# Graph layer kernel on one core: the x rows loaded tile by tile, the word matmuls, loads and slot branch in another order, and mix·W1 of three output tiles ahead of a branch and a correction

## The chip, the core and the metric

The kernel runs on one core of a Trainium2 chip. The metric is the device time of one execution in microseconds; less is better. Matmuls run on TensorE (PE), elementwise work on VectorE (DVE) and ScalarE (ACT), gathers by index are issued by GpSimd (POOL), and most DMAs by SyncE (SP).

## The reference, cut to what matters

N = 1354 nodes with H = 512 features; `adj` is a sparse 0/1 matrix with ones on the diagonal; 10,000 index pairs of which few hit an edge of `adj`.

```python
# layer 0: attention over adj; only pairs (sub, obj) that are edges get a score other than 0
q = (x[sub] @ Wq.T + bq);  k = (x[obj] @ Wk.T + bk)            # 8 heads of 64
scores = zeros.at[:, sub, obj].set((q * k).sum(-1) / 8);  scores = where(adj == 0, -inf, scores)
scores[:, i, i] = 1e-7
x = layernorm(x + (softmax(scores).sum(0) / 8) @ x)
# layer 1: a graph convolution
x = layernorm(x + adj @ (x @ W1) + b1)
```

## The kernel before

Rows are taken in T = 11 tiles of 128 (the last has 74 rows). Nearly every softmax row is uniform, so layer 0 is a neighbour sum `adj @ x` scaled per row, and the few pairs that are edges (at most 64 "slots") are corrected by a small branch of work. All engines run lists written out by hand; semaphores join them. The stages are these.

**Loads.** SP issues the tiles of `adj_t` (704 KB each) into a ring of three in `stage`; load t waits until the cast of tile t−3 is done (`adj_cast`). ACT casts each to fp16 (`cast_adj`, L622). x comes in three loads of three tiles and two of one. SP also waits for `edges_split` (from DVE's `split_left`), stores the left-over pair indices to DRAM, waits until they are stored, and loads them again broadcast over the partitions (`hot`, `cols`). POOL meanwhile looks up the first LOOKED = 44 of 80 pair columns in `adj`, one gather each.

**Words and sums.** For each tile, `words(t)` on PE (L1116, 11 matmuls of 129 columns) packs the adjacency bits and counts the neighbours; DVE's `fold(t)` (L773 to L778) takes them out of PSUM and `coefs(t)` makes scale factors. `words(t)` waits for the cast of tile t and, since it has two banks, for fold t−2. `sum_neighbours(i)` (L1125, 22 matmuls of 512 columns) sums tile i. On DVE `add_sums(i)` (L849 and the moments L793, L794) takes it; ACT takes the root (L627), then casts two more adjacency tiles, then normalises (L658) and scales (L661); DVE makes the low half (`low_x1`, L862), and scale and shift (`scale_shift_of`, L798, L799). A turn i of ACT's loop thus has the casts 4+2i and 5+2i between the root and the normalisation of tile i. In the first two sums PE works in blocks of three x tiles as x arrives.

**Looks and picks.** After the last sums, `look(n)` (PE, L1139) multiplies a table with 500 pairs; `pick(n)` (DVE, L812) takes it; a look waits for the pick two before it. `select` (L1188) sums the picks into one word for each pair.

**Mix and the slot branch.** `mix_rows(a, b)` is x1ᵀ·adjᵀ (L1179): 12 units of 11 rows, a row being two matmuls, of 512 columns in the units 0 to 7 and of 330 in 8 to 11. Between its rows stand by hand the PE steps of the slot branch: numbering, compaction (L1212), spread (L1217), transposes of gathered rows, projections (L1234), dots, `scores_spread` (L1252), `mixed` (L1256), the transposes of the change (L1260) and the change times W1 (L1267). DVE and ACT do the small steps between. ACT evicts a mix unit (`mix_high`, L666), DVE makes its low half (`mix_low`, L818).

**Branch and output.** All engines load `count_i` into a register and branch over a general path that is not taken (L248). Then `transform` (L1279: 12 matmuls mix·W1; L1287: 2 of the correction) makes the output tiles over six banks; DVE and ACT normalise them and SP stores them.

## Time and profile before

| | |
|---|---|
| median of 3 runs | 214.2 us (212.41 to 219.76) |
| the profiled execution | 212.14 us, of which the span from first to last instruction is 210.4 |
| PE busy | 175.6 us (83%) |
| DVE / ACT / POOL busy | 119.9 / 70.0 / 75.6 us |
| mean granted TensorE clock | 0.929 |

```profile
PE   4489720999999999969999999997589699999920
DVE  2569505776777677794621571059984226556660
ACT  6376123578533333370211111108022101332350
PEclk9958955699999999999999999999799999999995
DMA  5993299998798899120110060000000001122220
```

Each digit is a fortieth of the span (5.3 us), in tenths of busy time; PEclk is the granted clock, 5 being the lower of its two levels (1.2 GHz) and 9 about the upper (2.4 GHz). PE is busy nearly all the time except in the slices 5 to 7, a stretch near 145 to 157 us, and the end.

### The profile page before, as it was taken

Reading aid. Unit: us, or ns where it says so; the run is one execution under the profiler, and the core shown is the slowest. Engines: PE = TensorE matmul, PEld = TensorE weight load, DVE = VectorE, ACT = ScalarE, POOL = GpSimd, SP = SyncE. Lnnn points to the kernel's source line nnn. Section 1 sums busy time; section 2 is a strip of 40 time slices with the busy share of each in tenths; the row PEclk is TensorE's granted clock in tenths of the full one; section 3 lists DMA queues with packets and bytes.
Section 4 is the critical chain, followed back from the end, with each engine's and each line's share of the span. In section 5 each row is a group of like instructions: output and inputs, shape, how many; then the busy total and the mean of one; then the engine's idle time right before and its main releaser. Section 6 shows DMA issues by size and latency. Waiting matters only on the chain.

```text
span 210.4 us, 2793 instructions
## 1 busy us (share of the span) xinstructions
PE 175.6 (83%) x995; PEld 94.6 (45%) x995; DVE 119.9 (57%) x371; ACT 70.0 (33%) x119; POOL 75.6 (36%) x87
## 2 busy tenths in 40 slices
PE   4489720999999999969999999997589699999920
PEld 4444320655555444435444446954255344444520
DVE  2569505776777677794621571059984226556660
ACT  6376123578533333370211111108022101332350
POOL 5687887878785562301882150000000000000000
PEclk9958955699999999999999999999799999999995
DMA  5993299998798899120110060000000001122220
GB/s 162 377 346 82 29 379 332 310 341 201 174 324 272 292 289 309 52 52 3 1 1 1 0 181 9 0 3 2 0 0 0 5 9 50 65 86 100 97 106 29
DMA packets 14594, 26.66 MB, mean 127 GB/s; under 512 B 5459, under 2 KB 5620, under 8 KB 14445
## 3 DMA queue, kind: packets, MB, share of 16 engines
q1 hardware_dynamic: 9436, 22.46, 31.9%
q10 hardware_dynamic: 3152, 2.90, 4.5%
q0 software_dynamic: 1984, 1.05, 4.0%
q8 instruction: 10, 0.16, 0.3%
q14 instruction: 12, 0.09, 0.2%
HBM read 16.70 MB, written 9.65 MB: 125 GB/s over the span
## 4 chain that ended last, share of the span: by engine, by line
PE 65%; DVE 17%; DMA 7%; ACT 4%; issue 3%; SPq 1%; ACTq 0%; DVEq 0%
PE acc L1179 18%; PE acc L1125 14%; PE acc L1279 10%; PE tr L1125 7%; DMA x_sb<-in_x 5%; PE tr L1116 3%; PE tr L1234 3%; PE tr L1279 2%; DVE xs L766 2%; DMA stage<-in_adj_T 2%; DVE st L793 2%; PE acc L1287 2%; ACT adjT L622 1%; PE tr L1267 1%; PE acc L1188 1%
## 5 line engine op out<-in xcount | busy, mean ns | idle before, releaser
L570 POOL DMA_INDIRECT ed_adj<-in_adj,ed_idx x44 | 55.2, 1255 | 19.0 <-issue 16.0
L1179 PE MATMUL acc<-adjT,x1s 128*128 128x512 f16 (+3 forms) x264 | 54.3, 360 | 0.0
L1125 PE MATMUL acc<-xs,adjT 128*128 128x512 f16 (+1 forms) x176 | 41.3, 392 | 0.7 <-DVE xs L766 0.7
L1179 PEld LDWEIGHTS acc<-adjT,x1s 128*128 128x128 f16 (+1 forms) x264 | 25.5, 100 | 24.6 <-issue 1.8
L1125 PEld LDWEIGHTS acc<-xs,adjT 128*128 128x128 f16 (+1 forms) x176 | 17.4, 100 | 21.5 <-DVE xs L766 1.8
L1279 PE MATMUL acc<-whl,xs 128*128 128x512 f16 (+1 forms) x108 | 23.5, 367 | 2.1 <-issue 2.1
L1116 PE MATMUL tr<-bit_eye,adjT 128*128 128x129 f16 x121 | 11.5, 260 | 12.8 <-ACT adjT L622 12.8
L666 ACT ACTIVATE xs<-acc 128x512 f16<-128x512 f32 (+1 forms) x12 | 6.5, 546 | 43.5 <-PE acc L1179 43.5
L622 ACT CAST adjT<-stage 128x1408 f16<-128x1408 f32 x11 | 14.9, 1363 | 12.6 <-DMA stage<-in_adj_T 12.3
L1116 PEld LDWEIGHTS tr<-bit_eye,adjT 128*128 128x128 f16 x121 | 9.9, 118 | 15.6 <-ACT adjT L622 10.9
L1279 PEld LDWEIGHTS acc<-whl,xs 128*128 128x128 f16 x108 | 10.5, 98 | 13.9 <-issue 2.4
L587 POOL DMA_INDIRECT found<-in_adj,top_i x8 | 10.6, 1323 | 15.5 <-DVE top_i L904 13.3
L1125 PE MATMUL tr<-xs,adjT 128*128 128x512 f16 (+1 forms) x66 | 15.6, 394 | 0.0
L818 DVE SCALAR_TENSOR_TENSOR xs<-acc,xs 128x512 f16<-128x512 f32 (+1 forms) x12 | 7.4, 624 | 10.8 <-ACT xs L666 10.6
L627 ACT ACTIVATE st<-st,co 128x1 f32<-128x1 f32 x11 | 3.2, 293 | 22.2 <-DVE st L794 22.1
L1125 PEld LDWEIGHTS tr<-xs,adjT 128*128 128x128 f16 (+1 forms) x66 | 6.6, 102 | 8.0 <-issue 1.1
L766 DVE SCALAR_TENSOR_TENSOR xs<-x_sb,xs 128x512 f16<-128x512 f32 x11 | 6.9, 685 | 4.0 <-ACT xs L632 4.0
L711 ACT ACTIVATE y<-y,st 128x512 f32<-128x512 f32 x6 | 4.9, 812 | 12.3 <-DVE st L799 12.3
L793 DVE BATCH_NORM_STATS2 st<-y 128x6 f32<-128x512 f32 x12 | 8.3, 694 | 0.4
L1073 DVE SCALAR_TENSOR_TENSOR y<-acc,x_sb 128x512 f32<-128x512 f32 x5 | 3.5, 691 | 8.7 <-PE acc L1287 8.7
L627 ACT ACTIVATE st<-st,eps 128x1 f32<-128x1 f32 x13 | 3.7, 283 | 12.8 <-DVE st L794 12.6
L862 DVE SCALAR_TENSOR_TENSOR x1s<-x_sb,x1s 128x512 f16<-128x512 f32 x11 | 7.5, 681 | 0.4 <-ACT x1s L661 0.4
(236 smaller groups left out, 209.2 us busy)
## 6 DMA issues: line engine op xcount, KB each, us to landing
stage<-in_adj_T SPq DMA_DIRECT2D x11, 704.0 KB, 7.7
adjT_dram<-adjT SPq DMA_DIRECT2D x11, 352.0 KB, 3.0
x_sb<-in_x SPq DMA_DIRECT2D x3, 768.0 KB, 11.5
sums_dram<-y ACTq DMA_DIRECT2D x6, 256.0 KB, 5.9
out<-y SPq DMA_DIRECT2D x6, 256.0 KB, 2.0
sums_dram<-xd ACTq DMA_DIRECT2D x5, 256.0 KB, 3.3
hot<-row_dram SPq DMA_DIRECT2D x1, 1125.0 KB, 8.8
stage<-in_L_gnn_weight SPq DMA_DIRECT2D x1, 1024.0 KB, 6.5
```

Source lines behind the costliest of these rows:

```text
L570: nc.gpsimd.indirect_dma_start(out=ed_adj[0:EP, c:c + 1], out_offset=None, in_=adj_flat, in_offset=bass.IndirectOffsetOnAxis(ap=ed_idx[0:E ...
L587: nc.gpsimd.indirect_dma_start(out=found[0:EP, c:c + 1], out_offset=None, in_=adj_flat, in_offset=bass.IndirectOffsetOnAxis(ap=top_i[0:EP, ...
L622: nc.scalar.copy(adjT[:, :, t * P:(t + 1) * P], stage[:, t % RING, :].rearrange("p (k i) -> p k i", k=T)).then_inc(adj_cast, 1)
L627: return nc.scalar.activation(s[:, 10:11], s[:, 7:8], ACT.Sqrt, bias=floor)
L766: V.scalar_tensor_tensor(xs[:, 1, t, :], x_sb[:, t, :], XS, xs[:, 0, t, :], ALU.mult, ALU.subtract).then_inc(x_lo, 1)
L793: step(V.bn_stats(s[:, 0:6], v))
L818: V.scalar_tensor_tensor(mix[:, 1, u % KF, i:j], mix_bank(u)[:, 0:j - i], 1.0 / XS, mix[:, 0, u % KF, i:j], ALU.mult, ALU.subtract).then_i ...
L862: V.scalar_tensor_tensor(x1s[:, 1, i, :], x_sb[:, i, :], XS, x1s[:, 0, i, :], ALU.mult, ALU.subtract).then_inc(x1_lo, 1)
L1116: last = mm(tr[t % 2][:, 0:P + 1], adjT[:, k, t * P:(t + 1) * P], bit_eye[:, k, :], start=(k == 0), stop=(k == T - 1))
L1125: last = mm(sum_bank(i)[:, :], adjT[0:width[k], k, i * P:(i + 1) * P], xs[0:width[k], half, k, :], start=(k == 0 and half == 0), stop=(k = ...
L1179: ins = mm(mix_bank(u)[:, 0:j - i], x1s[0:width[k], half, k, f * P:(f + 1) * P], adjT[0:width[k], k, i:j], start=(k == 0 and half == 0), s ...
L1279: mm(bank, mix[:, a, k, t * P:(t + 1) * P], whl[:, b, k, columns], start=(k == 0 and n == 0), stop=False)
```

## The change

- x is loaded in 11 single tiles, and the load of the left-over pairs goes behind x and adjacency tile 2. The adjacency loads 3, 4 and 5 no longer stand behind SP's wait for `edges_split`; tile 6 stands behind it, tile 7 behind the `hot` broadcast.
- DVE makes all 11 low halves of x, then folds and coefs of tiles 0 and 1, then `split_left` and `edge_bits`, then the loop. Fold 2 moves into turn 0, folds 3 and 4 into turn 2, and so on (`FOLDS_AFTER`); `low_x1(i-1)` comes before `scale_shift_of(i)`.
- PE runs words 2 before the sums of tile 2, words 3 and 4 before those of 3, 5 and 6 before 4, and so on (`WORDS_BEFORE`).
- LOOKED goes from 44 to 40, so that 40 pair columns are left over (before 36), 10 looks instead of 9 and 40 selects instead of 36. Two looks each follow the sums of tiles 7, 8 and 9; four stand in the mix rows, each two rows apart.
- The slot branch: some mix rows stand elsewhere between its PE steps; the part of the DVE chain that needs only `gsub` (through the moments of `kk`) moves ahead of the scores, its root with it, so that ACT loads the Exp table before the scores are there and no mix unit's eviction stands between; the scaling by `rep` moves to the two-element coefficients.
- `transform` becomes `base` (mix·W1) and `correct`; the base of output tiles 0, 1 and 2 runs before the branch over the general path, and the general path (not taken) clears and remakes them.

```diff
-LOOKED = 44
+LOOKED = 40
-LOOKS_AFTER = {T - 4: range(0, 1), T - 3: range(1, 3), T - 2: range(3, 5), T - 1: range(5, 6)}
+WORDS_BEFORE = {2: (2,), 3: (3, 4), 4: (5, 6), 5: (7,), 6: (8, 9), 7: (10,)}
+FOLDS_AFTER = {0: (2,), 2: (3, 4), 3: (5, 6), 4: (7,), 5: (8, 9), 6: (10,)}
+LOOKS_AFTER = {T - 4: range(0, 2), T - 3: range(2, 4), T - 2: range(4, 6)}
+LOOKS_IN_MIX = {2: 6, 4: 7, 6: 8, 8: 9}
+EARLY = 3
...
             load_adj(0)
-            for g in range(3):
-                if g == 1:
-                    load_adj(1)
-                sp.dma_start(x_sb[:, 3 * g:3 * g + 3, :],
...
+            for t in range(3):
+                load_x(t)
+            load_adj(1)
+            for t in range(3, T):
+                load_x(t)
             load_adj(2)
+            sp.dma_start(left_i, pairs_left).then_inc(left_loaded, 16)
+            load_adj(3)
+            load_adj(4)
+            load_adj(5)
             sp.wait_ge(edges_split, 2)
...
-            load_adj(3)
-            load_adj(4)
+            load_adj(6)
             sp.wait_ge(row_stored, 16)
             sp.dma_start(hot[:, :], row_dram.partition_broadcast(P)).then_inc(row_spread, 16)
-            load_adj(5)
+            load_adj(7)
...
             for i in range(T):
                 add_sums(i)
-                if i + LEAD + 1 < T:
-                    fold(i + LEAD + 1)
-                if i + 2 < T:
-                    coefs(i + 2)
-                scale_shift_of(i)
+                for t in FOLDS_AFTER.get(i, ()):
+                    fold(t)
+                if 1 <= i < T - 1:
+                    coefs(i + 1)
                 if i >= 1:
                     low_x1(i - 1)
+                scale_shift_of(i)
...
             last.then_inc(keys_ready, 1)
-            mix_high(7)
+            act.wait_ge(slot_moments, 1)
+            root(st[:, 0], eps[:]).then_inc(slot_root, 1)
 
             nc.scalar.activation(table_loader[:, 1:2], eps[:], ACT.Exp)
             act.wait_ge(exps_in, 1)
             nc.scalar.activation(score, score, ACT.Exp).then_inc(exps_done, 1)
             nc.scalar.activation(table_loader[:, 2:3], eps[:], ACT.Sqrt)
+            mix_high(7)
             mix_high(8)
-            act.wait_ge(slot_moments, 1)
-            root(st[:, 0], eps[:]).then_inc(slot_root, 1)
...
-            mix_rows(118, UNITS * T)
-
-            with overflow(pe):
-                general_pe(pe)
+            mix_rows(117, UNITS * T)
...
+            for t in range(EARLY):
+                pe.wait_ge(mix_lo, (4, 4, 9)[t])
+                base(out_bank(t)[:, :], t, everything).then_inc(based, 1)
+
+            with overflow(pe):
+                general_pe(pe, base)
```

On PE, at the start of the sums (`tr<-bit_eye,adjT` is a tile's words, `xs,adjT` a tile's sums of 22 matmuls), before:

```order
L1125 MATMUL acc<-xs,adjT 128x512 x38
L1116 MATMUL tr<-bit_eye,adjT 128x129 x44
L1125 MATMUL tr<-xs,adjT 128x512 x22
L1116 MATMUL tr<-bit_eye,adjT 128x129 x11
L1125 MATMUL acc<-xs,adjT 128x512 x22
L1116 MATMUL tr<-bit_eye,adjT 128x129 x11
L1125 MATMUL acc<-xs,adjT 128x512 x22
```

The same place of the changed kernel:

```order
L1131 MATMUL acc<-xs,adjT 128x512 x38
L1122 MATMUL tr<-bit_eye,adjT 128x129 x11
L1131 MATMUL tr<-xs,adjT 128x512 x22
L1122 MATMUL tr<-bit_eye,adjT 128x129 x22
L1131 MATMUL acc<-xs,adjT 128x512 x22
L1122 MATMUL tr<-bit_eye,adjT 128x129 x22
L1131 MATMUL acc<-xs,adjT 128x512 x22
```

Four tiles' words stood between the first sums and those of tile 2; now one does, and the others stand one or two sums later.

On PE, around the branch over the general path (`whl,onehot` is the change times W1, `whl,xs` 12 matmuls of mix·W1, `stackR,stackL` the correction), before, with the general path left out between the two pieces:

```order
L1267 MATMUL tr<-whl,onehot 64x512 x12
L1179 MATMUL acc<-adjT,x1s 128x330 x28
L248 TENSOR_LOAD count_i
L248 ISA x2
L248 COMPARE_AND_BRANCH
L277 UNCONDITIONAL_BRANCH
```

```order
L1272 UNCONDITIONAL_BRANCH
L1279 MATMUL acc<-whl,xs 128x512 x12
L1287 MATMUL acc<-stackR,stackL 128x512 x2
L1279 MATMUL tr<-whl,xs 128x512 x12
L1287 MATMUL tr<-stackR,stackL 128x512 x2
```

The changed kernel ahead of the branch, and behind it:

```order
L1270 MATMUL tr<-whl,onehot 64x512 x12
L1183 MATMUL acc<-adjT,x1s 128x330 x30
L1279 MATMUL acc<-whl,xs 128x512 x12
L1279 MATMUL tr<-whl,xs 128x512 x12
L1279 MATMUL acc<-whl,xs 128x512 x12
L252 TENSOR_LOAD count_i
L252 ISA x2
L252 COMPARE_AND_BRANCH
```

```order
L1299 UNCONDITIONAL_BRANCH
L1291 MATMUL acc<-stackR,stackL 128x512 x2
L1291 MATMUL tr<-stackR,stackL 128x512 x2
L1291 MATMUL acc<-stackR,stackL 128x512 x2
L1279 MATMUL acc<-whl,xs 128x512 x12
```

36 matmuls of 512 columns moved ahead of the register load and the branch; none was added on the path that is taken.

## Rows read from the trace of the kernel before

**Rows 1.** The page: the span.

```profile
span 210.4 us, 2793 instructions
```

**Rows 2.** Waits of PE: waiting line, awaited, us in total, times, longest.

```profile
PE tr L1116 <- ACT adjT L622: 12.8, 3, 5.3
...
PE tr L1139 <- DVE hot L812: 2.2, 2, 1.7
PE acc L1279 <- issue: 2.1, 1, 2.1
```

**Rows 3.** Timeline of SP: start us, us, what was issued.

```profile
23.54 0.32 SPq L510 DMA_DIRECT2D row_dram<-row  x1
...
24.32 0.83 SPq L497 DMA_DIRECT2D stage<-in_adj_T  x2
25.19 0.42 SPq L515 DMA_DIRECT2D hot<-row_dram  x1
```

**Rows 4.** Chain that ended last: start us, us, what.

```profile
28.48 1.37 ACT adjT L622
...
39.25 5.56 PE tr L1125 x22
44.81 0.65 PE tr L1116 x11
45.46 4.75 PE acc L1125 x22
```

**Rows 5.** Timeline of PE: the last words before the gap.

```profile
24.40 0.81 PE L1116 MATMUL tr<-bit_eye,adjT 128*128 128x129 f16 x11
```

**Rows 6.** Busy time in a stretch: PE, PEld, DVE, ACT, POOL, then clock, DMA share, GB/s.

```profile
145.00:157.00 12.00, 7.59 (x37) 3.79 (x36) 11.03 (x34) 3.29 (x8) 0.00 (x0) 0.86 0.00 0
```

**Rows 7.** DMA issues: KB each, us from issue to landing.

```profile
hot<-row_dram SPq DMA_DIRECT2D x1, 1125.0 KB, 8.8
```

**Rows 8.** Timeline of ACT: casts, a root, a normalisation.

```profile
20.69 1.37 ACT L622 CAST adjT<-stage 128x1408 f16<-128x1408 f32 x1 [0.60 <-DMA stage<-in_adj_T]
50.32 0.81 ACT L658 ACTIVATE x_sb<-xd,st 128x512 f32<-128x512 f32 x1
51.17 0.63 ACT L661 ACTIVATE x1s<-x_sb 128x512 f16<-128x512 f32 x1
```

**Rows 9.** Timeline of DVE: first and last of the 14 instructions of one turn.

```profile
50.24 0.75 DVE L849 SCALAR_TENSOR_TENSOR xd<-acc,co,x_sb 128x512 f32<-128x512 f32 x1 [1.39 <-PE acc L1125]
...
54.17 0.61 DVE L805 TENSOR_SCALAR hot<-hot,row_no 128x1500 f16<-128x1500 f16 x1
```

**Rows 10.** Timeline of PE: the long stretch of mix rows.

```profile
96.27 19.60 PE L1179 MATMUL acc<-adjT,x1s 128*128 128x512 f16 x90
```

**Rows 11.** Timeline of ACT: the Exp table and the Exp of the scores.

```profile
143.52 1.28 ACT L685 ACT_TABLE_LOAD   x1
...
144.92 0.63 ACT L687 ACTIVATE wraw<-wraw 128x536 f32<-128x536 f32 x1
```

**Rows 12.** Timeline of DVE: scores done, and the sum behind the Exp.

```profile
143.35 0.72 DVE L997 TENSOR_TENSOR wraw<-wraw 128x536 f32<-128x536 f32 x1
...
146.66 0.65 DVE L1019 TENSOR_REDUCE wraw<-wraw 128x8 f32<-128x512 f32 x1
```

**Rows 13.** Timeline of PE: the end of the slot branch, and the mix rows before the branch instruction.

```profile
149.43 1.55 PE L1256 MATMUL tr<-wraw 64*128 64x512 f32 x2 [3.48 <-DVE wraw L1031]
...
156.87 0.46 PE L1260 MATMUL tr<-ident,wraw 64*128 64x64 f32 x4 [0.93 <-DVE wraw L1050]
...
161.75 4.10 PE L1179 MATMUL acc<-adjT,x1s 128*128 128x330 f16 x28
```

**Rows 14.** Instructions of the branch: engine, ns min/median/max, start us.

```profile
L248 SPq COMPARE_BRANCH  x1: 50/50/50, 120.5 to 120.5; - x1
...
L248 PEldq TENSOR_LOAD <-count_i x1: 483/483/483, 163.2 to 163.2; - x1
...
L248 PEldq COMPARE_BRANCH  x1: 3845/3845/3845, 164.0 to 164.0; - x1
```

More of the change, by code:

```diff
@@ L325, in general_pe @@
             pe.wait_ge(turn, FINISHED)
+            for t in range(EARLY):
+                base(out_bank(t)[:, :], t, slice(0, H))
         def general_act(act):
@@ L640, in _ @@
             cast_adj(0)
-            high_x(0)
+            for t in range(3):
+                high_x(t)
             cast_adj(1)
-            high_x(1)
-            high_x(2)
-            high_x(3)
-            for t in range(2, LEAD + 1):
-                cast_adj(t)
+            for t in range(3, T):
+                high_x(t)
+            cast_adj(2)
+            cast_adj(3)
             for i in range(T):
@@ L652, in _ @@
                 act.dma_start(sums_dram[i * P:(i + 1) * P, 0:H], y4(i)).then_inc(y_stored[i % YS], 16)
-                for t in range(LEAD + 1 + 2 * i, min(LEAD + 3 + 2 * i, T)):
+                for t in range(4 + 2 * i, min(6 + 2 * i, T)):
                     cast_adj(t)
@@ L671, in _ @@
             nc.scalar.mul(bias_hl[:, 0], bias_row[:, :], WS).then_inc(bias_split, 1)
-            for u in range(7):
+            for u in range(6):
                 mix_high(u)
@@ L827, in _ @@
             step(V.scalar_tensor_tensor(diag_bit, aii_all, -1.0, power, ALU.mult, ALU.mult))
[L828 removed]
+            for t in range(T):
                 split_x(t)
[L830 to L837 removed]
+            for t in range(2):
+                fold(t)
+                coefs(t)
             split_left()
[L839 to L840 removed]
             edge_bits()
@@ L880, in _ @@
                     pick(n)
+            pick(LOOKS_IN_SUMS)
             low_x1(T - 1)
-            for n in range(LOOKS_AFTER[T - 1].stop, LOOKS):
+            for n in range(LOOKS_IN_SUMS + 1, LOOKS):
                 pick(n)
@@ L964, in _ @@
             V.tensor_copy(xoT, tr[2][:, 0:KF * SLOTS]).then_inc(xoT_ready, 1)
+            dve.wait_ge(gsub_in, 16)
+            aii = gsub[:, H + 1:H + 2]
+            plain, off = slot[:, 7:8], slot[:, 9:10]
+            step(V.tensor_tensor(off, gsub[:, H:H + 1], aii, ALU.subtract))
+            b = small[:, 24:32]
+            own, den, both = b[:, 0:1], b[:, 1:2], b[:, 2:3]
+            step(V.tensor_scalar(own, aii, -A0, 1.0, ALU.mult, ALU.add))
+            step(V.tensor_scalar(den, off, A0, 1.0, ALU.mult, ALU.add))
+            step(V.tensor_tensor(both, den, own, ALU.add))
+            step(V.reciprocal(b[:, 3:4], den))
+            step(V.tensor_tensor(b[:, 4:5], both, b[:, 3:4], ALU.mult))
+            step(V.tensor_scalar(kk, gsub[:, 0:H], b[:, 4:5], None, ALU.mult))
+            norm_a, norm_b = st[:, 0], st[:, 1]
+            moments(norm_a, kk).then_inc(slot_moments, 1)
             mix_low(6)
@@ L976, in _ @@
             last.then_inc(qk_read, 1)
+            dve.wait_ge(slot_root, 1)
+            step(scale_shift(norm_a))
+            step(V.tensor_scalar(norm_a[:, 8:10], norm_a[:, 8:10], rep, None, ALU.mult))
+            V.tensor_scalar(kk, kk, norm_a[:, 8:9], norm_a[:, 9:10], ALU.mult, ALU.add).then_inc(dve_step, 1)
+            steps += 1
             sc = small[:, 4:12]
@@ L1153, in _ @@
             sum_neighbours(1, range(9, T))
-            for t in range(2, LEAD + 2):
-                words(t)
             for i in range(2, T):
-                if i + LEAD < T:
-                    words(i + LEAD)
+                for t in WORDS_BEFORE.get(i, ()):
+                    words(t)
                 if i >= 3:
@@ L1190, in select @@
                     last.then_inc(selected, 1)
-            looks = LOOKS_AFTER[T - 1].stop
-            mix_rows(0, 2)
-            for n in range(looks, LOOKS):
-                look(n)
-                mix_rows(2 * (n - looks) + 2, 2 * (n - looks) + 4)
-            for n in range(looks):
+            for n in range(9):
+                mix_rows(n, n + 1)
+                if n in LOOKS_IN_MIX:
+                    look(LOOKS_IN_MIX[n])
+            for n in range(LOOKS_IN_SUMS):
                 select(n)
-            mix_rows(2 * (LOOKS - looks) + 2, 9)
-            for n in range(looks, LOOKS):
+            mix_rows(11, 13)
+            for n in range(LOOKS_IN_SUMS, LOOKS):
                 select(n)
-            mix_rows(11, 20)
+            mix_rows(13, 20)
             mix_rows(9, 11)
@@ L1222, in _ @@
             last.then_inc(xobj_T, 1)
-            mix_rows(77, 78)
+            mix_rows(73, 76)
             pe.wait_ge(xsub_in, 16)
```

106 lines of the change are left out of this document (44 added, 62 removed).

## The prediction

> **What bounds the kernel now.** I read the page's slices first, then the waits of PE, then the chain that ended last. The execution took 212.14 us, of which the span is 210.4 [rows 1]; the 1.74 us around it I keep. PE is busy in almost every slice outside a few holes, and the chain runs mostly over PE, so a hole closed is time won, as long as no other engine takes its place. The largest waits in the table are 12.8 us for ACT's casts (three of them), 2.2 us for DVE's picks and 2.1 us of "issue" before the first output tile [rows 2]. The timeline of PE adds 3.48 and 0.93 us late in the slot branch [rows 13].
>
> The casts are late because of SP's list, not because of the bus. SP has adjacency tile 3 behind its wait for the split pairs: it stores them at 23.54, so tile 3 is issued only at 24.32 [rows 3] and cast at 28.48 [rows 4], while tile 2 was cast at 20.69 [rows 8]. Tile 4's cast stands on ACT behind the root of tile 0, and that root waits for DVE, which must first fold tile 3. PE did words 2 from 24.40 [rows 5] and began the sums of tile 2 at 39.25, and those took 5.56 us where the later ones take 4.75 [rows 4].
>
> **The first gap: -13.5 us.** In the new list tiles 3 to 5 don't wait for the split, and only words 2 stands ahead of the sums of tile 2. From 24.40 to 39.25 are 14.85 us; in them lay four tiles' words, which are still to be done and cost 0.65 us each at the full clock [rows 4], 2.6 in all. That leaves 12.25. The sums of tile 2 come at 4.75 instead of 5.56: 0.8. Single x tiles let the first products start earlier; the first sums of 38 matmuls were bound by PE, so this is small: I take 0.5, with 0 and 1 as ends.
>
> **What is late next: +4.4 us.** The cover of 13 us is gone, and now the loads are asked for earlier than they can come. A load of 704 KB issued on an idle queue landed in 4.1 us (24.32 to the cast at 28.48). Two such loads and the 1125 KB of `hot` were done 8.8 us after 25.19 [rows 3, 7], at 34.0: the 1829 KB behind tile 3 took 5.5 us, about 330 KB/us. So an adjacency tile takes 2.1 us, and `hot`, now 1250 KB, 3.8. Tile 2 at 20.7, tile 3 at 22.8, tile 4 at 24.9, tile 5 at 27.0, tile 6 (issued near 25, behind the split) at 29.1, `hot` at 33, tile 7 behind it at 35.1. Two stores of 256 KB that ACT issues meanwhile take 0.8 each: 36.7.
>
> Tile 7's cast stands on ACT between root 1 and the normalisation of tile 1. It ends near 38.1; normalisation and scaling, 0.81 and 0.63 [rows 8], bring 39.6. On DVE `low_x1(1)` now stands ahead of scale and shift of tile 2, so the DVE list stands still: queued behind it are add_sums 3 and folds 5 and 6. A turn of DVE is 4.5 us (50.24 to the end of the row at 54.17 [rows 9]) and PE's turn 5.4, so DVE makes up only about 1 us a turn, less where two folds stand in one. By these steps PE, which would be at words 7 at 41.3, waits for fold 5 until 42.9 (1.6); at words 9 for fold 7 (1.4); at look 0 for the table, which now comes in turn 6 (1.3). Together about 4.4. The slope is 1 us for each us that tile 7 lands later; if it lands by 32.5 there is no wait at all. Ends: 0 and +9 (tile 7 and its followers 4 to 5 us later, as when the stores and the broadcast of `cols` share the bus).
>
> **Looks: -0.9.** Four looks in the mix rows stand one row further apart. The last waits for the pick two before it, which stands behind `low_x1(10)`: 1.0 of wait in place of 2.2. One look and four selects more cost 0.3. The flags must be back from POOL when PE has done the mix rows behind the selects; two rows fewer lie there (0.43 each: 19.60 us for 90 matmuls [rows 10]), which the earlier end of the selects pays. Four lookups fewer lie beside this work and cost or give nothing.
>
> **Slot branch: -3.3.** The scores are written at 143.35 + 0.72 = 144.1, but Exp started at 144.92, since the table load began only at 143.52 [rows 11, 12], behind the eviction of mix unit 7. DVE then did the `gsub` part and reached the sum at 146.66. Now both lie in the cover of the projections: Exp from 144.1, 0.63 long, the sum at 144.8, 1.9 earlier. PE had 3.48 us of wait there [rows 13] to take it from. From L1256 to L1260 are 7.4 us [rows 13], set by DVE; three passes over 512 elements leave that chain and small ones come in: -1.0, between -0.5 and -1.5. One mix row less stands ahead of the spread of scores: -0.4. The clock was 0.86 from 145 to 157 [rows 6], after the long wait; waits of 1.4 and 1.3 us remain, shorter than the 2.1 [rows 2] behind which the outputs ran at full pace, so I expect the upper level, 2.4 GHz. This changes no sum here, since DVE sets it.
>
> **Bases ahead of the branch: -2.0.** The wait of 2.1 before L1279 is the branch. TensorE's sequencer loaded the register at 163.2, while matmuls ran until 165.85 (161.75 + 4.10), and its branch instruction lasted 3845 ns from 164.0 [rows 13, 14]; SP's took 50 ns [rows 14]. So load and branch need 4.7 us, of which 2.65 were covered by about 18 queued matmuls of 0.146 us. Ahead of them now are matmuls of 0.216 us: the same 18 cover 3.9, a gap of 0.8. In longer matmuls the sequencer gains more lead, and 36 of them, 7.8 us, stand there; I take the gap as 0.1. Ends: 2.1 won or nothing. The outputs 0 to 2 then come in a bunch, later for DVE, but DVE's part of an output (add, moments, scale and shift) is a piece of its turn of 4.5 us [rows 9], an estimated 2, against PE's 14 matmuls of 0.216, 3.0, and there are six banks; what follows the last output matmul stays as it is.
>
> The Trainium skill ("Runtime: NRT & Kernel Launch", Instruction fetch mechanics) says that a taken branch to a target outside the fetched pages must wait for a DMA of the target page. A fetch would run beside queued matmuls; by that rule, which the row of 3845 ns bears out, the gap goes and the sum stands.
>
> **The sum.** 212.14 - 13.5 + 4.4 - 0.9 - 3.3 - 2.0 = 196.8 us. The median of the runs before is 2.1 above the profiled execution and the lowest run 0.3 above it; I leave the number as it is.
>
> **Rivals.** *No late wait*: tile 7 lands by 33. For it: loads before tile 2 were asked for in one go. Against: the 330 KB/us and 1250 KB of `hot` ahead of it. 196.8 - 4.4 = 192.4. *The branch waits for an empty array*: its 3845 ns end 2.04 after the last matmul, which fits that as well. Then nothing is won: 198.8. *A longer wait of DVE*: tiles 7 to 9 come 4 to 5 us later: 201 to 203. *Slower than before*: DVE's `split_left` now waits for the pairs, whose load stands behind x and tile 2, and behind it stand add_sums 0 and the whole list. By the same rate they land at 21, when DVE gets there; each us beyond it costs one. From 15 us late the gain of 15.3 is gone; at 24 us late it would be 196.8 + 24 = 220.8. Nothing in the rows speaks for such a delay of so small a load.
>
> **Chances and range.** Forecast 0.52; no late wait 0.15; branch not covered 0.17; longer DVE wait 0.12; slower 0.01; and 0.03 that gains are lost in places I don't see, to within 2% of before (about what a measurement of this kernel can tell from no change). Faster by over 2% is thus 0.95, within 0.03, slower 0.02. The forecast alone spans 194.5 to 199. From 191.5 to 203 leaves out less than 2 in 10: the low end is no late wait with the better start, the high end the longer wait of DVE.
>
> **What would show it.** Right: PE without a hole from 24 to 41 us, then waits for `fold_in` and for the table of 1 to 2 us each; a cast of ACT near 37 that waited for its load; the sums' end near 78 (before 87); Exp within 0.1 us of the scores; the wait before L1256 about 1.4; the branch instruction of TensorE as long as before, with no hole in the matmuls beside it. Wrong: waits of PE for casts again, a hole of 2 us right behind the bases, or waits of 3 us and more for DVE in the sums.

## The result, and the profile after

The changed kernel takes 202.6 us (median of 4 runs, 201.5 to 204.6), the kernel before beside it 217.0 (median of 4 runs, 212.4 to 220.4); the ratio is 0.948, 95% interval 0.933 to 0.963. The medians in this text contain executions that were slower whatever the kernel did, and the ratios leave them out: without them the kernel before shows about 213. Faster, as forecast, but 5.8 us above the 196.8 that was predicted, at the upper end of the range. The profiled execution took 201.47 us:

```profile
span 199.7 us, 2808 instructions
```

The waits of PE (columns as in [rows 2]). The 12.8 us for ACT's casts are 0.6 now. Besides 2.9 us for POOL at the start, which both kernels have, the largest that are left are the fold in the sums, DVE's split of the last x tile, the two of the slot branch and the branch itself:

```profile
PE tr L1122 <- DVE fold_in L786: 3.6, 1, 3.6
...
PE acc L1131 <- DVE xs L778: 2.6, 2, 1.8
PE tr L1259 <- DVE wraw L1040: 1.6, 1, 1.6
PE tr L1263 <- DVE wraw L1056: 1.5, 1, 1.5
PE tr L1145 <- DVE hot L824: 1.0, 1, 1.0
PE acc L1291 <- issue: 0.8, 1, 0.8
PE tr L1122 <- ACT adjT L634: 0.6, 2, 0.4
```

The timeline of PE in the sums, and from their end (79.17) to the numbering, PE's first step for the slots (L1209, at 110.18). L1122 are words, L1131 sums, L1183 mix rows, L1145 looks, L1192 selects:

```profile
20.61 1.75 PE L1131 MATMUL acc<-xs,adjT 74*128 74x512 f16 x6 [1.75 <-DVE xs L778]
22.74 1.37 PE L1122 MATMUL tr<-bit_eye,adjT 128*128 128x129 f16 x11 [0.38 <-ACT adjT L634]
23.90 5.50 PE L1131 MATMUL tr<-xs,adjT 128*128 128x512 f16 x22
...
45.13 1.02 PE L1122 MATMUL tr<-bit_eye,adjT 128*128 128x129 f16 x11 [3.64 <-DVE fold_in L786]
45.94 6.42 PE L1131 MATMUL tr<-xs,adjT 128*128 128x512 f16 x22
...
84.99 0.37 PE L1145 MATMUL tr<-hot,table 128*128 128x500 f16 x1 [1.00 <-DVE hot L824]
85.20 1.53 PE L1192 MATMUL acc<-ones,hot 128*125 128x1 f16 x24
86.59 1.87 PE L1183 MATMUL acc<-adjT,x1s 128*128 128x512 f16 x4
88.25 1.81 PE L1192 MATMUL acc<-ones,hot 128*125 128x1 f16 x16
89.93 20.41 PE L1183 MATMUL acc<-adjT,x1s 128*128 128x512 f16 x86
110.18 0.17 PE L1209 MATMUL acc<-flag,below 125*128 125x8 f16 x1
```

The same two places in the kernel before, in its timeline of PE (what follows the last sums there is a look):

```profile
86.95 0.38 PE L1139 MATMUL tr<-hot,table 128*128 128x500 f16 x1
...
115.70 0.17 PE L1206 MATMUL acc<-flag,below 125*128 125x8 f16 x1
```

Sums 2 begin at 23.90, where they began at 39.25 [rows 4], and PE is through with the sums 7.8 us earlier (79.17; before 86.95). Then it loses 2.3 of them again: 31.0 us to the numbering where it took 28.8. The stretches (columns as in [rows 6]) say why; the clock fell to its lower level, 1.2 GHz, around the selects. PE is busy throughout these four; just ahead of them, at 84, lies its wait of 1.0 us:

```profile
86.00:88.00 2.00, 2.00 (x17) 1.17 (x16) 0.92 (x3) 0.00 (x0) 0.00 (x0) 0.63 0.04 8
88.00:90.00 2.00, 2.00 (x19) 1.80 (x18) 0.00 (x0) 0.00 (x0) 0.00 (x0) 0.50 0.00 0
90.00:92.00 2.00, 2.00 (x6) 0.64 (x6) 1.56 (x8) 0.00 (x0) 0.00 (x0) 0.50 0.00 0
92.00:94.00 2.00, 2.00 (x8) 0.80 (x7) 0.97 (x9) 0.00 (x0) 1.16 (x1) 0.66 0.00 0
```

The timeline of ACT: the cast of the last x tile (the one before it is cast at 14.99), and of adjacency tile 7.

```profile
19.20 0.63 ACT L643 ACTIVATE xs<-x_sb 128x512 f16<-128x512 f32 x1 [3.58 <-DMA x_sb<-in_x]
...
39.29 1.36 ACT L634 CAST adjT<-stage 128x1408 f16<-128x1408 f32 x1 [5.77 <-DMA stage<-in_adj_T]
```

The timeline of SP: three adjacency loads hold it from 9.16 until 23.04, since tile 5 waits for the cast of tile 2. The stores of the split pairs come at 25.04 ([rows 3] has 23.54), and the broadcast into `hot` at 27.90:

```profile
25.04 0.31 SPq L523 DMA_DIRECT2D row_dram<-row  x1
...
27.90 0.34 SPq L527 DMA_DIRECT2D hot<-row_dram  x1
```

What the stores waited for from 23.04 on is DVE's split, and `hot` waited for the stored rows (SP's waits, columns as in [rows 2]):

```profile
SPq L523 <- DVE col L765: 2.0, 1, 2.0
SPq L527 <- DMA row_dram<-row: 1.8, 1, 1.8
```

DVE's timeline has the reason: its split stands behind the low half of the last x tile, for whose cast it sat idle for 3.51 us; the split's last instruction (L765) ends at 25.01.

```profile
19.86 0.69 DVE L778 SCALAR_TENSOR_TENSOR xs<-x_sb,xs 128x512 f16<-128x512 f32 x1 [3.51 <-ACT xs L643]
```

### The profile page after: what moved, and what is told of

It is laid out like the page before. It is cut to its first block, busy times and chain, and to the rows that moved or that the text cites. A ratio compares the mean times of both kernels' runs of the same rounds, so it can differ in the third digit from the quotient of the medians.

```text
span 199.7 us, 2808 instructions
## 1 busy us (share of the span) xinstructions
PE 176.2 (88%) x1000; PEld 94.4 (47%) x1000; DVE 120.0 (60%) x373; ACT 70.0 (35%) x119; POOL 71.3 (36%) x83
## 4 chain that ended last, share of the span: by engine, by line
PE 62%; DVE 18%; DMA 6%; issue 6%; SPq 3%; ACT 3%; DVEq 0%
PE acc L1183 20%; PE acc L1279 10%; PE acc L1131 10%; DMA x_sb<-in_x 6%; PE tr L1131 5%; PE tr L1237 4%; PE tr L1279 3%; DVE st L805 2%; SPq L509 2%; PE acc L1291 2%; PE acc L1192 1%; PE tr L1122 1%; PE tr L1270 1%; DVE xd L854 1%; DVE x1s L867 1%
## 5 line engine op out<-in xcount | busy, mean ns | idle before, releaser
L582 POOL DMA_INDIRECT ed_adj<-in_adj,ed_idx x40 | 50.1, 1252 | 18.8 <-issue 15.7
L1183 PE MATMUL acc<-adjT,x1s 128*128 128x512 f16 (+3 forms) x264 | 55.6, 365 | 0.0
L1131 PE MATMUL acc<-xs,adjT 128*128 128x512 f16 (+1 forms) x176 | 40.1, 381 | 2.6 <-DVE xs L778 2.6
L1183 PEld LDWEIGHTS acc<-adjT,x1s 128*128 128x128 f16 (+1 forms) x264 | 25.6, 101 | 25.2 <-issue 4.2
L1131 PEld LDWEIGHTS acc<-xs,adjT 128*128 128x128 f16 (+1 forms) x176 | 16.7, 98 | 22.8 <-DVE xs L778 4.2
L1131 PE MATMUL tr<-xs,adjT 128*128 128x512 f16 (+1 forms) x66 | 16.8, 417 | 0.0
L599 POOL DMA_INDIRECT found<-in_adj,top_i x8 | 11.4, 1423 | 12.5 <-DVE top_i L910 10.4
L1122 PE MATMUL tr<-bit_eye,adjT 128*128 128x129 f16 x121 | 9.6, 238 | 4.2 <-DVE fold_in L786 3.6
L1122 PEld LDWEIGHTS tr<-bit_eye,adjT 128*128 128x128 f16 x121 | 8.5, 107 | 6.9 <-ACT adjT L634 5.9
L1131 PEld LDWEIGHTS tr<-xs,adjT 128*128 128x128 f16 (+1 forms) x66 | 7.1, 108 | 8.8 <-issue 2.7
L643 ACT ACTIVATE xs<-x_sb 128x512 f16<-128x512 f32 x11 | 6.6, 624 | 4.3 <-DMA x_sb<-in_x 4.1
```

Of the source, the lines that this page charges most:

```text
L582: nc.gpsimd.indirect_dma_start(out=ed_adj[0:EP, c:c + 1], out_offset=None, in_=adj_flat, in_offset=bass.IndirectOffsetOnAxis(ap=ed_idx[0:E ...
L599: nc.gpsimd.indirect_dma_start(out=found[0:EP, c:c + 1], out_offset=None, in_=adj_flat, in_offset=bass.IndirectOffsetOnAxis(ap=top_i[0:EP, ...
L1122: last = mm(tr[t % 2][:, 0:P + 1], adjT[:, k, t * P:(t + 1) * P], bit_eye[:, k, :], start=(k == 0), stop=(k == T - 1))
L1131: last = mm(sum_bank(i)[:, :], adjT[0:width[k], k, i * P:(i + 1) * P], xs[0:width[k], half, k, :], start=(k == 0 and half == 0), stop=(k = ...
L1183: ins = mm(mix_bank(u)[:, 0:j - i], x1s[0:width[k], half, k, f * P:(f + 1) * P], adjT[0:width[k], k, i:j], start=(k == 0 and half == 0), s ...
```

## The experiments

All are edits of the changed kernel unless said otherwise. A bracket behind a time holds its ratio to the kernel before and the 95% interval of that ratio; 0.010 is about 2 us. Where two times are compared across chips, their ratios to the kernel before are the better guide; the medians of it beside them were 212.7 to 218.6.

**The changed kernel again**, as the base for the runs beside it.

> The changed kernel as it is, as the measure for the runs beside it. Theory: span near 199.7 as in its first profile (201.5 us), with one wait of PE of 3.6 us for a fold in the sums, and the granted clock at its lower level for about 7 us around the selects (86 to 94 us in the first profile). Rival: the clock fell there by chance; then this run shows the upper level there and 3 us less from the last sums to the numbering (31.0 us in the first profile, 28.6 in the kernel before).

Measured 201.9 us (0.947, 0.938 to 0.955), so some 202. Its profiled execution repeats the fold wait (3.3), the split wait (2.8), both waits of the slot branch and the low clock at the selects.

**The last x tile in two loads, of 64 and 10 rows.**

```
- sp.dma_start(x_sb[0:width[t], t, :], rows(x, t))           # t = 10: 74 rows
+ sp.dma_start(x_sb[0:64, t, :], x[t*P:t*P+64, :]); sp.dma_start(x_sb[64:LAST, t, :], x[t*P+64:N, :])
```

> One edit: the last x tile, of 74 rows, is loaded in two pieces, of 64 and of 10 rows. Theory: its load ran on 2 of the 16 DMA engines (the Trainium skill, 'DMA: Bandwidth & Descriptors', says that the number of engines is the largest up to 16 that divides the rows: 2 for 74, 16 for 64, 10 for 10), which is why it landed at 19.2 us, 4 us behind the tile before it; now it lands by 16.5, PE's wait of 1.8 us before the last rows of the first sums goes, and adjacency tile 2 is cast 2 us or more earlier. Since the later wait for tile 7 is set by the queue, 0 to 2 us of it show at the end. Rival: it is late because it is last in the queue: it lands at 18.5 or later again, no change.

Measured 198.0 us (0.931, 0.921 to 0.940), profiled 196.04. ACT's timeline: both last x tiles are cast at 15.00 in one go, tile 2 at 17.47, tile 7 at 35.96:

```profile
15.00 1.26 ACT L647 ACTIVATE xs<-x_sb 128x512 f16<-128x512 f32 x2 [0.60 <-DMA x_sb<-in_x]
17.47 1.36 ACT L638 CAST adjT<-stage 128x1408 f16<-128x1408 f32 x1 [1.21 <-DMA stage<-in_adj_T]
...
35.96 1.36 ACT L638 CAST adjT<-stage 128x1408 f16<-128x1408 f32 x1 [5.36 <-DMA stage<-in_adj_T]
```

In SP's timeline of this run the stores of the split pairs stand at 21.88 and the broadcast into `hot` at 24.61.

So one load of 148 KB had delayed everything behind it: on ACT the cast of tile 2, on DVE the low half of the last x tile and the split behind it, with that the stores (25.04 to 21.88) and `hot`, by 3.3 us. From the issue of `hot` to the cast of tile 7 it takes 11.4 us in either kernel (39.29 - 27.90, 35.96 - 24.61). The Trainium skill ("DMA: Bandwidth & Descriptors", Why a DMA increments its semaphore by 16 and not by 1) says that a transfer runs on the largest number of engines up to 16 that divides its outermost size: 2 for 74 rows, 16 for 64. The trace agrees: the same bytes in pieces of 64 and 10 rows are cast 3.6 us earlier (15.63 against 19.20). In the five kernels of this study with the split tile its cast starts at 15.6 to 17.0, in the other eleven that were changed at 18.8 to 20.3. That the gain comes from the number of engines and not from there being two loads, no run separates. The end of the sums is 2.2 us earlier in this profiled execution (76.96); the rest of the 5.4 us between 201.47 and 196.04 is mostly that the clock did not fall at the selects here.

The fold wait doesn't shrink, though, since PE is earlier by as much (PE's timeline):

```profile
41.79 0.82 PE L1126 MATMUL tr<-bit_eye,adjT 128*128 128x129 f16 x11 [3.34 <-issue]
```

**The small load of the left pairs at the head of SP's list** instead of behind tile 2.

```
+ sp.dma_start(left_i, pairs_left)
  load_adj(0)
  ...
  load_adj(2)
- sp.dma_start(left_i, pairs_left)
```

> One edit: the load of the left-over pairs (40 rows of 1 KB) stands ahead of adjacency tile 0 again, as in the kernel before. It asks why adjacency tile 0 was cast at 8.3 us in the kernel before and at 5.3 to 5.9 in the changed one. Theory A: this small load delays the tile behind it by 3 us: the cast comes at 8 us again. Theory B: it was the x load of three tiles behind it: the cast stays below 6.5 us.

A single execution, 202.25 us. Tile 0 was cast at 7.72 instead of 5.29, and words 0 followed at 9.23 (7.09). The fifteen profiled executions without these 39 KB ahead of it have that cast at 5.29 to 6.93, so they cost the first tile 0.8 to 2.4 us. The kernel before has 8.33, so this is a large part of why the changed kernel starts earlier than I had priced.

**Adjacency tile 7 ahead of the broadcast of the rows.**

```
  load_adj(6)
+ load_adj(7)
  sp.wait_ge(row_stored, 16)
  sp.dma_start(hot, ...)
- load_adj(7)
```

> One edit: adjacency tile 7 is issued ahead of the broadcast of the left-over pairs instead of behind it. Theory: PE's wait of 3.6 us for a fold, and the lower clock behind it (1.5 us on the sums of tile 5), come from the cast of tile 7 that stands on ScalarE ahead of a normalisation and waited for its load until 39.3; now the load lands near 33, the wait goes, and the time is 4 to 5 us less. Rival: the bus is full, and the broadcast, now 2 us later, or tiles 8 and 9 hold DVE and PE as long: within 1 us of the changed kernel.

Measured 202.5 us (0.953, 0.948 to 0.958): no gain, as the rival had it. Tile 7 was cast at 36.72, 2.6 us earlier, but tile 8 only at 46.32, and the wait went there. PE's timeline:

```profile
54.85 1.35 PE L1122 MATMUL tr<-bit_eye,adjT 128*128 128x129 f16 x11 [5.80 <-DVE fold_in L786]
55.99 7.28 PE L1131 MATMUL acc<-xs,adjT 128*128 128x512 f16 x22
```

**Both broadcasts behind adjacency tile 9** (on top of the split x tile).

```
- load_adj(6); store rows, then hot; load_adj(7); cols; load_adj(8), load_adj(9), load_adj(10)
+ load_adj(6), load_adj(7), load_adj(8), load_adj(9); hot; cols; load_adj(10)
```

> Two edits on the changed kernel: the last x tile in two loads (as x10_split) and the two broadcasts of the left-over pairs issued behind adjacency tile 9 instead of around tile 7. Theory: the queue is full from 24 to 46 us, and what counts is which load stands first; with both broadcasts behind, tiles 7 to 9 land 3 to 6 us earlier, the wait of PE for a fold (3.3 us) goes and the lower clock behind it, so it is 3 to 5 us below x10_split. Rival: DVE then waits for the broadcast in turn 3 (before turns 3 to 5 use it), and the lists stand as long: within 1 us of x10_split or above it.

Measured 197.8 us (0.924, 0.913 to 0.935), the same as with the split x tile alone. Tiles 7, 8 and 9 were cast at 33.62, 36.45 and 39.34, tile 10 after a wait of 5.14 at 47.41, and PE waited 2.50 for the fold behind it. Moving bytes about in SP's list moves the wait; it doesn't remove it.

**ACT's casts behind the normalisation**, on top of three other edits (the kernel `best_so_far`, below): in every turn (first), and in all turns but 0 (second).

```
  root(i)
- cast_adj(4 + 2 * i), cast_adj(5 + 2 * i)
  normalise x1(i), scale x1s(i)
+ cast_adj(4 + 2 * i), cast_adj(5 + 2 * i)      # second: only for i > 0
```

> best_so_far with ACT's casts of a turn moved behind the normalisation and scaling of that turn, so that a cast that waits for its load no longer holds up the low part, DVE and its fold. Theory A (the wait of 3.3 us for fold 5 comes from ACT's order: DVE idles about 5 us on low_x1(1) while the cast waits): the wait goes, 3 us less than best_so_far, 193.5. Theory B (the loads are late on their own account and PE has used up its reserve of work): the fold wait shrinks by 1 at most and comes back as a wait for words 8 or 9, same time as best_so_far. A cast that stands 1.5 us later on ACT delays words by up to 1.5 us; that is the price in either.

> best_so_far with ACT's casts behind the normalisation in turns 1 to 3 only; in turn 0 tiles 4 and 5 are cast first, as in the changed kernel. Theory A (the fold wait of 3.1 to 3.6 us comes from the cast of tile 7 standing ahead of the normalisation, and the wait of 2.5 for cast 4 in norm_first from the cast standing behind it): neither wait, and the sums behind at full clock, 3 to 4 us less than 193.9: 190. Theory B (the loads of tiles 7 to 10 are what is late): the wait comes back before words 7 or 8, and the time stays within 1 of 193.9.

The first form measured 193.8 us (0.911, 0.905 to 0.918), against 194.0 of its base: no gain in time. The fold wait of 3.1 is gone, so it did come from ACT's order: in the changed kernel DVE stands idle 5.36 us ahead of `low_x1(1)` (42.07), which needs the scaling that ACT did behind the cast of tile 7. But cast 4 now stands behind the normalisation of turn 0, and that opened a wait of its own, with the low clock behind it:

```profile
28.54 1.06 PE L1130 MATMUL tr<-bit_eye,adjT 128*128 128x129 f16 x11 [2.48 <-ACT adjT L642]
29.39 6.39 PE L1139 MATMUL acc<-xs,adjT 128*128 128x512 f16 x22
```

The second form measured 193.0 us (0.907, 0.898 to 0.915), which can't be told from the first by these runs; I had expected 190. In PE's timeline no sums ran at the lower clock any more, but waits came back piecemeal, 4.1 us in three: 1.35 for a cast ahead of the words at 27.56, 0.96 and 1.77 for folds ahead of those at 40.55 and 48.53.

**The first gap, half undone twice**: SP's list as before from tile 3 on (`pairs_first`), and three tiles' words ahead of sums 2 on PE (`words_early`; the kernel before has four).

```
- load_adj(3), load_adj(4), load_adj(5); stores; load_adj(6); hot; load_adj(7); cols; load_adj(8) ...
+ stores; load_adj(3), load_adj(4); hot; load_adj(5); cols; load_adj(6) ...          # pairs_first
```

```
- WORDS_BEFORE = {2: (2,), 3: (3, 4), 4: (5, 6), 5: (7,), 6: (8, 9), 7: (10,)}
+ WORDS_BEFORE = {2: (2, 3, 4), 3: (5,), 4: (6,), 5: (7,), 6: (8, 9), 7: (10,)}     # words_early
```

> The changed kernel with SP's list as before from adjacency tile 3 on: tiles 3 and 4 behind the stores of the split pairs, tile 5 behind the broadcast of the rows, 6 to 10 behind that of the columns. PE's, ACT's and DVE's orders stay as changed. Prediction's theory (the casts were late because of SP's list): most of the 13.5 us comes back; at least 8 us slower than the changed kernel, 210. Rival (it was the order of the words on PE: sums 2 no longer stand behind words 3 to 6): tile 3 is cast at about 28.5, when sums 2 end anyway, tile 4 at about 32, so a wait of 3 us before sums 3 and 1 to 2 before sums 4, while the late wait for fold 5 goes: 0 to 3 us slower, 202 to 205.

> The changed kernel with words 2, 3 and 4 ahead of the sums of tile 2, then one tile's words ahead of each of sums 3 to 5, as the kernel before had it at the start; SP's list as changed. Theory A (the order of the words carries most of the 13.5 us): words 4 can't start before cast 4, at 29.4 in the changed kernel, or before fold 2, which DVE does behind add_sums 0; so sums 2 start at about 30.5 in place of 23.9, but they then stand behind three tiles' words that were due anyway (1.3 us): 5 us slower, 207; the wait for fold 5 shrinks, which gives back up to 3. Theory B (the list alone had carried it): less than 1.5 us slower.

Measured 206.0 us (0.973, 0.963 to 0.983) and 203.3 us (0.954, 0.946 to 0.961), against 202 of the changed kernel. The prediction's sentence "the casts are late because of SP's list" falls for the most part: with the old list sums 2 still start at 22.86, and PE waits 5.8 us ahead of words 3 and 4, and 2.18 for a fold at 45.42 (`pairs_first`):

```profile
22.86 4.91 PE L1129 MATMUL tr<-xs,adjT 128*128 128x512 f16 x22
31.99 1.37 PE L1120 MATMUL tr<-bit_eye,adjT 128*128 128x129 f16 x11 [4.23 <-ACT adjT L632]
34.91 1.37 PE L1120 MATMUL tr<-bit_eye,adjT 128*128 128x129 f16 x11 [1.55 <-ACT adjT L632]
```

With the words early and the new list, sums 2 start at 31.84 behind cast 4 (wait 4.29), and then one wait of 2.18 at 40.03 stands in place of the 3.64. Undoing the list costs 4 us (5 by the ratios), the words about 1, which these intervals can't tell from nothing; what either costs early is in part paid back late. Either one of the two thus closes most of the gap. No run undoes both at once, so that the two together carry the 13.5 us is argued, not shown.

**The selects**, set apart in the mix rows four by four (`selects_apart`), and all forty in a row (`selects_row`).

```
  for n in range(6): select(n)                  # 24 one-column matmuls
- mix_rows(11, 13)                              # selects_row: these rows behind the second group
  for n in range(6, 10): select(n)              # 16
```

```
+ mix_rows(n, n + 1); look(...); select(n)      # selects_apart, n = 0 to 5
+ mix_rows(5 + n, 6 + n); select(n)             # n = 6 to 9
```

> One edit: the 40 selects (matmuls of one column) stand in ten groups of four, each behind a mix row, instead of as 24 and 16 with two rows between. Theory: the lower clock around 86 to 94 us came from the selects standing together right behind a wait; apart, it stays at the upper level and the time is 3 us less. Rival 1: the clock fell for the wait of 1.0 us before the last look alone: no change. Rival 2: chance: it varies from run to run in both kernels.

> The changed kernel with the two mix rows between the two groups of selects moved behind them: 40 one-column matmuls in a row. Theory A (a string of one-column matmuls keeps the array so little busy that the clock falls): the granted clock falls to the lower level right behind or in them in each profiled execution; from the sums' end to the numbering 31 us or more, where it was 28.0 without a fall and 26.5 with the selects apart; the time 1 us above the changed kernel, which has the fall in most executions already: 203. Theory B (the wait of 1.0 before look 9 does it, which all have): no difference from the changed kernel, 28 to 31 us by the execution.

Measured 198.9 us (0.934, 0.928 to 0.940) and 200.6 us (0.940, 0.925 to 0.954). Set apart they save some 3 us. From the sums' end to the numbering all profiled executions give:

| selects | executions | sums' end to numbering |
|---|---|---|
| in groups, clock falls | after, changed_again, adj7_first, words_early | 31.0 each |
| in groups (selects_row: in one row), clock falls for less | hot_behind9, base_behind, load_hoisted, left_first, selects_row | 29.4 each |
| in groups, no fall | x10_split, pairs_first, chain_behind | 28.0 to 28.2 |
| apart, no fall | selects_apart, best_so_far, norm_first, norm_second | 26.5 each |

So the fall costs 3.0 or 1.4 us for the same instructions, and it was there in 9 of 12 executions with the selects in strings and in none of 4 with them apart. Apart, the stretch is another 1.5 us shorter (28.0 to 26.5), since the wait of 1.0 before the last look, which all twelve have, is gone too. In `selects_apart` the granted clock stays up:

```profile
90.00:92.00 2.00, 2.00 (x21) 1.33 (x20) 1.02 (x3) 0.00 (x0) 0.00 (x0) 1.00 0.04 8
```

The row of forty came out as its theory B had it, not theory A: the clock fell behind it (0.50 from 90 to 92), but the stretch was 29.4, not 31, and the kernel was no slower. That the edit ends the fall is shown. Whether the string brings it or the wait of 1.0 us right ahead of it isn't, since `selects_apart` took both away. The kernel before had strings of 24 and 12 selects behind waits of 1.74 and 0.50, and its profiled execution has the full clock there:

```profile
94.00:96.00 2.00, 2.00 (x33) 1.80 (x32) 0.66 (x2) 0.00 (x0) 0.00 (x0) 1.00 0.04 8
```

Nor is it shown what makes one execution fall for longer than another, or not at all.

**The slot chain as before**: on ACT mix unit 7 ahead of the Exp table and the root behind unit 8, on DVE the `gsub` part and its scale and shift back behind the scores.

```
  keys_ready
- root(norm_a); load Exp table; Exp; load Sqrt table; mix_high(7); mix_high(8)
+ mix_high(7); load Exp table; Exp; load Sqrt table; mix_high(8); root(norm_a)
```

> The changed kernel with the slot chain as before in two places: on ACT mix unit 7 ahead of the Exp table load and the root of the first norm behind unit 8, on DVE the part on gsub (and its scale, shift and pass over kk) back behind the scores and the mixed term. PE's rows stay as changed. Prediction's theory: from the spread of scores to the transposes of dx1 16.2 us again in place of 13.6, so 2.6 to 3.3 slower: 205. Rival (what is taken from the chain is partly given back in the mix rows that no longer cover the next wait): only the two waits of PE grow, by 1 in all: 203.

Measured 203.0 us (0.953, 0.943 to 0.963), against 202.6 and 201.9: in the medians not to be told apart. In PE's timeline it is: from L1255 to L1263 13.6 us in the changed kernel (133.88 to 147.50), 17.2 here (131.84 to 149.02). The first wait doubles, and the clock is low behind it, 6.73 us for the 28 matmuls that take 4.10 in the changed kernel; so 1.8 of the 3.6 us more come ahead of L1259 and 1.8 behind it:

```profile
140.63 1.81 PE L1259 MATMUL tr<-wraw 64*128 64x512 f32 x2 [3.34 <-DVE wraw L1035]
142.37 6.73 PE L1183 MATMUL acc<-adjT,x1s 74*128 74x330 f16 x28
```

This execution had no fall at the selects (28.2), both profiled ones of the changed kernel did: 3.6 lost against 3.0 gained, which would explain medians that hardly differ, if the other executions are like these.

**The branch**: no bases ahead of it (`base_behind`, EARLY = 0), and its register load hoisted to ahead of the wait for the shares (L1259), where it reads the same count (`load_hoisted`).

```
- EARLY = 3
+ EARLY = 0                                     # base_behind
```

```
  mix_rows(85, 98)
+ found_count = value_load(count_i)             # load_hoisted
  pe.wait_ge(shares_ready, 1)
  ...
- with overflow(pe):                            # loads the register and branches
+ with pe.If(found_count > SLOTS):
```

> One edit: the mix*W1 matmuls of output tiles 0 to 2 stand behind the branch again. Theory: TensorE's branch instruction takes 3.7 us from its start whatever it follows, and about 18 queued matmuls cover part of it; with matmuls of 0.146 us ahead of it instead of 0.216 the hole is 2.1 us instead of 0.8, so the time is 1.3 us more. Rival 1: the hole is the same (the branch waits for an empty array): no change. Rival 2: the placement is worth all of 2.1.

> One edit: TensorE loads the count into a register ahead of the step L1259, some 25 us before the branch, instead of right ahead of it. Theory: the sequence at the branch is then 3.7 us instead of 4.6 and starts as far ahead of the array as before (about 18 matmuls of 0.216 us, 4.0 us): the hole of 0.8 us closes, 0.8 us less. Rival: the sequencer's lead shrinks with it and the hole stays.

Measured 200.9 us (0.940, 0.932 to 0.948) and 202.7 us (0.945, 0.933 to 0.957): in time neither differs from 202. The traces show the mechanism. Instructions of the branch in the changed kernel, columns as in [rows 14]:

```profile
L252 PEldq TENSOR_LOAD <-count_i x1: 488/488/488, 160.2 to 160.2; - x1
...
L252 PEldq COMPARE_BRANCH  x1: 3686/3686/3686, 161.1 to 161.1; - x1
```

and in PE's timeline, also of the changed kernel:

```profile
161.50 2.75 PE L1279 MATMUL acc<-whl,xs 128*128 128x512 f16 x12
165.06 0.59 PE L1291 MATMUL acc<-stackR,stackL 128*128 128x512 f16 x2 [0.80 <-issue]
```

With the load hoisted, the branch alone is left at its place:

```profile
L1304 PEldq COMPARE_BRANCH  x1: 3356/3356/3356, 159.9 to 159.9; - x1
```

It ends at 163.3, matmuls run to 163.9, and the hole is gone. From the numbering to the end of the span the changed kernel takes 89.5 us and 89.2 in its second profile, `base_behind` 90.5 and `load_hoisted` 88.6. The sequencer's lead is the same count each time: 18 matmuls of 0.146 us before (2.65 us, [rows 13, 14]) and in `base_behind` (load at 153.1, matmuls to 155.7), 18.7 of 0.216 in the changed kernel (160.2 to 164.25) and with the load hoisted (159.9 to 163.94). In `base_behind` the first output matmul starts 1.70 us late, at 157.44, when the branch instruction ends (153.9 + 3.44). The Trainium skill ("TensorE: Matmul & The Clock Gate", the table of facts at its head) gives the engine's queue as 64 deep; these four rows show a lead of 18 to 19 matmuls at a register load or branch. I had only the first of them, and went by it too little.

**The edits together**: x tile split, selects apart, register load hoisted.

> Three edits on the changed kernel together: the 74-row x tile loaded in two parts (64 and 10 rows), the ten selects set apart in the mix rows, the register load of the branch hoisted ahead of the mixing matmul. Theory A (each removes a wait of its own): against the changed kernel -3.5 for x, -1.5 on average for the selects (3 in those executions where the clock falls there), -0.5 for the branch: 202.2 - 5.5 = 196.7, profiled about 194. Theory B (the clock's dip at the selects is a late effect of the starved start, since it was not there with x split): the selects give nothing on top of x split: 197.5 to 198, and the hoisted load nothing that can be measured. Both expect PE without a hole ahead of the corrections and no slice under 0.9 of the clock at the selects.

Measured 194.0 us (0.912, 0.905 to 0.918): 8 us below the changed kernel and 4 below the split x tile alone (198.0). The register load is worth 0.6 to 0.9 of these by the traces, so the selects gave their part too and theory B falls. With the casts as in `norm_second` it is 193.0, the fastest kernel of this study, 0.907 of the time before.

## Why the prediction was right or wrong

The forecast for the profiled execution can be laid beside the trace at three points: the sums' end, the numbering, the end of the span.

| | before | predicted | after |
|---|---|---|---|
| sums' end | 86.95 | 77.85 | 79.17 |
| sums' end to numbering | 28.75 | 27.85 | 31.01 |
| numbering to end of span | 94.7 | 89.4 | 89.5 |

**The step that failed is "Looks: -0.9"**: it came out as +2.3, which is 3.2 of the 4.7 us between 196.8 and the profiled 201.47. I took the one look and four selects more as 0.3 of work and never asked what a string of one-column matmuls, with a wait of 1.0 ahead of it, goes with on the clock. The sentence "I expect the upper level" was argued for the slot branch, where it held (28 matmuls of 330 columns in 4.10), and the selects were not looked at. 3.0 of the 3.2 are the clock: the same instructions took 28.0 us in the executions without the fall, 0.15 from the forecast, and with the selects apart it was in none of four. The clock also took 1.5 us behind the fold wait and 0.6 behind the wait for the last x tile. These 5.1 us of low clock stand nowhere in the sum, which priced waits and not what follows them.

**First gap, -13.5: right in the sum, wrong in the cause.** PE has no hole between 24 and 41. The prediction laid the late casts to SP's list and gave the order of the words no share in them. With the list undone most of the gap stays closed, and with the words half undone too: 4 and 1 us singly.

**Start, 0.5: 1.7** (words 2 at 22.74, before 24.40), in spite of a loss that I missed. Tile 0 comes 3 us earlier, much of it because 39 KB no longer stand ahead of it. But the last x tile, a load of its own of 74 rows as before, was cast 4.2 us behind the one before it; PE, which now gets there earlier, waited 1.75, and the clock was low at first for the sums of tile 2 (5.50 in the timeline, where the kernel before has 5.77 and the full clock gives 4.91; I had taken 0.8 off). I had looked for which queue the small loads stand in, not for how each is cut.

**Late waits, +4.4: right in what holds PE up, and roughly in the total.** Expected were 1.6, 1.4 and 1.3; what came was a single wait of 3.64 at fold 5 and 1.5 us of low clock in the sums behind it (6.42 against 4.91), 5.1 in all. A wait "of 3 us and more for DVE in the sums" was one of the prediction's own signs of being wrong. Tile 7 was cast at 39.3, not near 37. The failed term is the issue of `hot`: "tile 6 (issued near 25)" was 25.77, since DVE's split stood behind the 74-row tile, and SP then waited 1.8 us for the rows to be stored, a wait that was put at nothing, and issued `hot` at 27.90. The slope held roughly: tile 7 was 2.6 us later than forecast, and the wait, met by PE at 41.5 (forecast 41.3), was 2.0 longer. The two waits behind it didn't come; PE had lost in one what I had spread over three. With the 74-row tile split tile 7 came at 35.96, and PE at 38.5 instead, so that the wait stayed; that run, profiled at 196.04 in an execution without the fall at the selects, is in time the kernel that I had predicted, though with one wait of 3.34 and 1.7 of low clock behind it in place of three short waits.

**Slot branch, -3.3: right.** Exp starts at 137.32, 0.03 behind the scores; the waits are 1.56 and 1.47 where I said 1.4 and 1.3; L1255 to L1263 is 13.6, where it was 16.2 and my 1.9 and 1.0 give 13.3. Undone, it is 17.2, more than before, since the clock was low in that execution. The whole from the numbering to the end is 89.5 where 89.4 was forecast; that this agrees so closely is luck, as the bases gave 0.7 less than I took and the rest 0.6 more.

**Bases ahead of the branch, -2.0: -1.3.** The hole is 0.80, the value that I had worked out from "the same 18" and then put aside for "in longer matmuls the sequencer gains more lead". It does in time, not in count, and a count was what the rows had. The agreement to the digit is luck: in `changed_again` the branch instruction took 3.32 us instead of 3.69, and the hole was 0.53. The branch itself runs beside queued matmuls (its rival, an empty array, falls: 2.1 would have stayed, and in `load_hoisted` it ended 0.7 us before they did). The rule on taken branches that I cited fits TensorE's 3.3 to 3.85 us, but no run here shows a fetch, and the other engines' branches over the same path took 0.05 to 0.08. In time, `base_behind` at 200.9 isn't slower than the changed kernel, so this term stands on the traces alone.

The rivals: *no late wait* falls. *A longer wait of DVE*, 201 to 203, names the right time for the wrong reason: PE lost 5.1 us there, not 9. And a small slip: the chances as listed add up to 0.96 for faster and 0.01 for slower, not 0.95 and 0.02.

## What to carry to other kernels

When a hole is closed, price what now stands next by the whole chain that leads to it, down to how each load is cut: a 148 KB load of 74 rows cost 3 to 4 us of time, more than most edits gain. Price a wait of PE with the low clock that can follow it. Look at strings of tiny matmuls as at waits: put them between long ones, which was worth some 3 us here. And where the trace gives a count (18 matmuls of lead), use the count; a register load ahead of a branch can stand where a wait covers it (0.6 to 0.9 us in the traces, too little for the times to show).

## What was not expected of the hardware

- The clock fell to 1.2 GHz around 40 one-column matmuls behind a wait of 1.0 us: 0.63, 0.50, 0.50 and 0.66 granted in four stretches of 2 us in all of which PE was busy, 3.0 us lost. It isn't the same in each execution (31.0, 29.4 or 28.0 us for the same instructions, in kernels that differ elsewhere). Which of the two, string or wait, it needs, is open; waits of 1.56 and 1.47 us in the slot branch, with long matmuls behind them, cost nothing of the clock.
- After waits of 1.75, 2.48, 3.64 and 5.80 us the 22 matmuls of the next sums took 5.50, 6.39, 6.42 and 7.28 us in place of 4.91; behind waits of 1.35, 0.96 and 1.77 us in `norm_second` they took 4.91. The length of the wait alone doesn't decide: 2.46 us in `best_so_far` were followed by 4.91, 2.53 in `selects_apart` by 6.13.
- A load of 39 KB at the head of a list delayed the 704 KB behind it by 0.8 to 2.4 us (one execution against fifteen).
- A taken branch of TensorE lasted 3.3 to 3.85 us in each run; those of SP, ACT, DVE and POOL 0.05 to 0.08.
